# Unnormalised queries: the inverse query norm moves into the softmax's exponential and its bias, with new order words

## The reference, cut to what matters

```
q = l2norm(q) * qs;  k = l2norm(k) * ksc          # l2norm(t) = t / max(|t|, 1e-12), per token and head
q, k = rotary_xpos(q, k)                          # rotation and per-feature scale, linear in q and k
bq = q * 8.0                                      # QK_SCALE; windows of 64, keys of this and the window before
sim = where(mask, -finfo.max, einsum('bhwid,bhwjd->bhwij', bq, bk))
attn = softmax(sim);  out = einsum('bhwij,bhwjd->bhwid', attn, bv)      # 8 heads of 64 features
```

## Time and profile before

| what | value |
|---|---|
| median of three executions | 2480.55 us |
| range | 2479.12 to 2483.96 us |
| the profiled execution, first to last instruction | 2483.7 us |
| one pass with the pipeline full (997.9 to 1138.8 us) | 140.9 us |
| busy: PE, DVE, ACT, POOL | 1934.9, 1919.8, 1830.6, 1778.2 us |

### The profile page before, as it was taken

The page is one execution under the profiler, slowest core; times in us unless marked ns, Lnnn a source line. Parts: engine busy times, 40 slices in busy tenths (PEclk is TensorE's granted clock), DMA queues, the critical chain, the costliest instruction groups (busy, mean ns, idle before and its releaser), DMA issues.

```text
span 2483.7 us, 44331 instructions
## 1 busy us (share of the span) xinstructions
PE 1934.9 (78%) x15936; PEld 1113.3 (45%) x15936; DVE 1919.8 (77%) x3509; ACT 1830.6 (74%) x4051; POOL 1778.2 (72%) x1668
## 2 busy tenths in 40 slices
PE   2156788797878888797878879797888879787866
PEld 0013355353635445353635445363645445363634
DVE  3557797978879797988879797988879797977442
ACT  2255788787878878786878878797878878686634
POOL 1969595977959596977959596886959596883020
PEclk9767999999999999999999999999999999999978
DMA  4443423333434333434433333434433333330000
GB/s 163 123 120 98 112 74 104 98 96 103 103 111 104 100 89 95 102 90 115 104 107 95 107 86 91 106 91 116 112 106 95 106 88 91 102 90 9 6 5 9
DMA packets 116107, 231.27 MB, mean 93 GB/s; under 512 B 24880, under 2 KB 57648, under 8 KB 115632
## 3 DMA queue, kind: packets, MB, share of 16 engines
q1 hardware_dynamic: 115888, 228.44, 34.5%
HBM read 185.42 MB, written 42.99 MB: 92 GB/s over the span
## 4 chain that ended last, share of the span: by engine, by line
DVE 30%; PE 28%; ACT 19%; issue 12%; POOL 2%; DMA 1%; DVEq 0%; SPq 0%; POOLq 0%; ACTq 0%
DVE hs L617 9%; DVE m L885 5%; ACT late L850 3%; DVE kr L899 3%; ACT da L593 3%; DVE b_bank L889 3%; PE b_bank L341 3%; DVE f_bank L889 2%; PE b_bank L719 2%; PE f_bank L341 2%; DVE ss L872 2%; PE b_bank L764 2%; DVE mx L916 2%; PE f_bank L995 2%; PE f_bank L1001 2%
## 5 line engine op out<-in xcount | busy, mean ns | idle before, releaser
L617 DVE TENSOR_TENSOR_SCAN hs<-da,dbu 128x512 f32<-128x512 f32 x512 | 622.3, 1215 | 112.8 <-POOL dbu L645 85.4
L662 POOL TENSOR_TENSOR gy<-hs,bc 128x512 f32<-128x512 f32 x512 | 650.4, 1270 | 44.9 <-DVE hs L617 40.9
L645 POOL TENSOR_TENSOR dbu<-spread,bc 128x512 f32<-128x512 f32 x512 | 649.5, 1269 | 9.2 <-DMA spread<-steps 9.2
L593 ACT ACTIVATE da<-spread,rest 128x512 f32<-128x512 f32 x512 | 359.1, 701 | 163.3 <-DVE hs L617 143.9
L954 POOL TENSOR_TENSOR kr<-kr,rn 128x512 f32<-128x512 f32 x256 | 263.6, 1040 | 18.7 <-ACT rn L810 15.3
L693 PE MATMUL b_bank<-rest,h_t 128*128 128x512 f32 x384 | 225.1, 687 | 49.2 <-DVE kr L899 40.8
L693 PE MATMUL f_bank<-rest,h_t 128*128 128x512 f32 x384 | 217.4, 653 | 56.5 <-DVE kr L899 49.3
L570 PE MATMUL y_sum<-gy,rest 128*32 128x512 f32 x1024 | 144.2, 638 | 87.9 <-POOL gy L662 87.9
L341 PE MATMUL b_bank<-first,kr 128*128 128x128 f32 x768 | 131.7, 307 | 97.0 <-DVE kr L899 61.5
L341 PE MATMUL f_bank<-first,kr 128*128 128x128 f32 x768 | 125.1, 291 | 100.3 <-DVE kr L899 63.3
L1107 POOL TENSOR_TENSOR xs<-xs,v 128x512 f32<-128x512 f32 x16 | 18.9, 1184 | 229.6 <-ACT xs L336 229.6
(11 more groups left out here) (172 smaller groups left out, 4942.1 us busy)
## 6 DMA issues: line engine op xcount, KB each, us to landing
spread<-steps SPq DMA_DIRECT2D x256, 512.0 KB, 4.7
bc<-bc_rows SPq DMA_DIRECT2D x32, 512.0 KB, 6.8
steps<-k_t SPq DMA_DIRECT2D x32, 512.0 KB, 2.7
gate<-gates SPq DMA_DIRECT2D x32, 512.0 KB, 5.6
gates<-kr SPq DMA_DIRECT2D x16, 512.0 KB, 2.7
gates<-late SPq DMA_DIRECT2D x16, 512.0 KB, 3.4
sq<-in_x SPq DMA_DIRECT2D x16, 256.0 KB, 4.8
x<-in_x SPq DMA_DIRECT2D x16, 256.0 KB, 4.8
```

The source lines that it names most:

```text
L593: e.activation(da[:, :], spread[:, slot(b, s // 2), 0, :], ACT.Exp, scale=a_neg[:, s:s + 1]).then_inc(decayed.sem, 1)
L617: e.tensor_tensor_scan(hs[:, s % 2, :], da[:, :], dbu[:, s % 2, :], 0.0, ALU.mult, ALU.add).then_inc(scanned.sem, 1)
L645: e.tensor_tensor(dbu[:, s % 2, :], spread[:, slot(b, s // 2), 1, :], bc[:, s % 2, :], ALU.mult).then_inc(fed.sem, 1)
L662: e.tensor_tensor(gy[:, s % 8, :], hs[:, s % 2, :], bc[:, 2 + s % 2, :], ALU.mult).then_inc(read_out.sem, 1)
```

## The change

Queries are no longer multiplied by `rn` on POOL: the take list of `pool_attention` loses q0 to q3, and PE turns a query tile as soon as DVE's `add` (L899) has written it. The scores, and so the row maximum, are then too large by the query's norm over 8. ACT's exponential gets the inverse query norm as its per-partition scale. Its bias is a new tile `shift`, the negated maximum times the inverse norm, which DVE makes per head in a new `tensor_tensor` of 128x4 (both inputs and the output in SBUF; `shift` is a view of `lg`, by which name the order shows it). A new semaphore `shifted` takes the place of `peaked` before the exponential. DVE's attention stream has 8 steps more, POOL's 4 fewer, and all five order words are new.

```
 ORDER = {
     "pool": (
-        "F4 C1 A4 M1 B1 M1 B1 M2 B1 M1 B1 M2 B1 M1 B3 M1 A1 M1 A2 M1 B1 M1 A1 B1 M1 B2 M1 B1 A1 M2 B1 A1 B2 M4 A3 "
-        "M1 A1 M1 A1 M1 A1 M44"),
+        "F4 C1 A2 B1 M5 B2 M3 A1 M1 B3 M1 A1 M1 A1 B1 M1 A1 M1 B1 M1 A1 B1 M1 A1 M1 B3 M5 A1 M2 A1 M1 A2 M43"),
...
+                self.shift = self.lg[:, :, 0:NT]
...
-                self.rotated, self.added, self.normed = s("rotated", 16), s("added", 8), s("normed", 8)
+                self.rotated, self.added, self.normed = s("rotated", 16), s("added", 8), s("normed", 4)
+                self.shifted = s("shifted", 8)
...
-                    E.wait_ge(*w.normed(b, ROPE.index(take.lower())))
+                    E.wait_ge(*(w.normed(b, t) if kind == "K" else w.added(b, ROPE.index(take.lower()))))
...
-                E.wait_ge(*w.peaked(b, hd))
+                E.wait_ge(*w.shifted(b, hd))
...
                 for p in range(NT):
+                    n = ROPE.index(f"q{p}")
                     op = e.activation(w.pr[:, hd % 2, p, :], X[hd % 2][:, p * P:(p + 1) * P], ACT.Exp,
-                                      bias=w.mx[:, hd, p:p + 1])
+                                      bias=w.shift[:, hd, p:p + 1], scale=w.rn[:, n, hd:hd + 1])
...
                 e.tensor_reduce(w.mx[:, hd, :], X[hd % 2][:, :].rearrange("p (t k) -> p t k", t=NT), AX, ALU.max,
                                 negate=True).then_inc(w.peaked.sem, 1)
+                yield
+                E.wait_ge(*w.inverse(b, 2))
+                E.wait_ge(*w.peaked(b, hd))
+                inverse_q = w.rn[:, :, hd].rearrange("p (a k i) -> p k a i", a=2, k=2)[:, 0, :, :]
+                e.tensor_tensor(w.shift[:, hd, :].rearrange("p (a i) -> p a i", a=2),
+                                w.mx[:, hd, :].rearrange("p (a i) -> p a i", a=2), inverse_q, ALU.mult).then_inc(
+                    w.shifted.sem, 1)
+                yield
...
-            for take in "c0 q0 q1 v0 c1 k0 v1 k1 c2 q2 q3 v2 v3 c3 k2 k3".split():
+            for take in "c0 v0 c1 k0 v1 k1 c2 v2 v3 c3 k2 k3".split():
```

More of the change, by code:

```diff
@@ L44 @@
     "pe": (
[3 rows of a table removed]
[3 rows of a table added]
     "act": (
[4 rows of a table removed]
[4 rows of a table added]
     "dve": (
[4 rows of a table removed]
[4 rows of a table added]
     "pool": (
-        "F4 C1 A4 M1 B1 M1 B1 M2 B1 M1 B1 M2 B1 M1 B3 M1 A1 M1 A2 M1 B1 M1 A1 B1 M1 B2 M1 B1 A1 M2 B1 A1 B2 M4 A3 "
-        "M1 A1 M1 A1 M1 A1 M44"),
-    "sp": "M1 F2 M10 E1 M2 C1 M6 B1 M2 S1 M1 S2",
+        "F4 C1 A2 B1 M5 B2 M3 A1 M1 B3 M1 A1 M1 A1 B1 M1 A1 M1 B1 M1 A1 B1 M1 A1 M1 B3 M5 A1 M2 A1 M1 A2 M43"),
+    "sp": (
+        "M1 F2 M3 C1 M7 E1 M6 B1 M5 S3"),
 }
@@ L929, in dve_attention @@
             for hd in range(0, HEADS, 2):
[L930 to L933, removed]
+                yield from peak(hd)
+                yield from peak(hd + 1)
                 if hd:
```

## The result

The changed kernel takes 2677.7 us (median of 4, 2670.9 to 2678.9) against 2479.8 us. The ratio is 1.0784, with a 95% interval of 1.0767 to 1.0801. The profiled execution has a span of 2675.7 us. The forecast was slower, 2615 us with a range of 2495 to 2720, and the time lies in its upper part.

What follows compares the result with a forecast made beforehand. DVE and POOL were both held near their limit for 106 us of a 140.9 us pass. Product 41, wait 151, exponential 27, absorption -73 and relief -15 made +131 on 2484: 2615 us, range 2495 to 2720.

Steps and rivals of the forecast that it cites:

- the signs: What would show the forecast right or wrong: product duration, POOL's busy time and waits, exponential duration, rotation stretch and pass length.
- the 0.5 named: On DVE, beside POOL: the new product's mean would be 0.5 us or more if the forecast was right.
- the 0.8 of my value: On DVE: the new product's mean duration, 0.8 us, that goes with the wait of 0.65 us taken.
- 147 to 151: Whole pass: predicted length in us after the change, against 140.9 before.
- POOL's relief, 15 us gain: POOL: 128 normalisations go, 133 us of its time; only one per pass, behind the rotations, gives time back, 15 us.
- The product's own 41 us: DVE, between scans: 256 new 128x4 products at an undisturbed 0.16 us each add 41 us.
- Its wait, 151 us: DVE beside POOL: 232 products each wait 0.65 us for a POOL operation boundary; bounds 81 and 269 us.
- Rival (c): DVE heads: the product loses every boundary until POOL is dry, 190 to 290 us more, about 2740 us; chance 0.13.
- The exponential, 27 us: ACT: scale and bias per partition lengthen exponentials; L850's chain share grows 17 to 37 us, 27 taken; bounds 0 and 120.
- The absorption, 73 us: DVE's idle in a pass's first two parts takes up 5.0 us per pass, 73 us; bounds 49 and 99.
- the rotation stretch keeps its length: First 35 us of a pass, DVE busy 34.97 of 35.10: its length was to stay unchanged.
- The second way to the size: Gaps from scan 10 to 32: ten get products and grow, some 10 us per pass, less what POOL's idle returns.

Runs made afterwards that it cites:

- e1: Changed kernel with the DVE product replaced by a one-input copy of mx in the same place, exponential scale a column of ones: 2607.8 us, 1.050.
- e8: Changed kernel with the one-input copy for the product, constant exponential scale 1.0 and the order words of before: 2502.3 us, 1.0066.
- e6: Kernel before, all normalisations kept, plus the 128x4 DVE product of two SBUF tiles behind each row maximum, read as the exponential's bias: 2577.5 us, 1.0375.
- e7: Kernel before with a column of ones as the exponential's per-partition scale beside its bias: 2548.9 us, 1.0259.
- e3: Changed kernel, new order words kept, with the one-input copy for the product and constant exponential scale 1.0: 2572.8 us, 1.037.
- e2: Changed kernel with a constant exponential scale (0.0), the DVE product left as it is: 2663.8 us, 1.073.

## Why the prediction was right, and which terms were off

Its direction and its mechanism hold. Its sum has wrong sizes that partly cancel, and lacks a term. Each alone, in medians: relief -2, product +93, scale +64, which makes 2640 of 2484; the kernel with all three in the old order measures 2647, so they add up within 7 us, though the product's group is 26 us longer there than alone (159.6 against 133.5). The new words bring +31. In the prediction's terms that is 39 + 94 + 64 - 40 - 2 = +155, and 7 and 31 more make +193, where the forecast had 41 + 151 + 27 - 73 - 15 = +131. The wait was put 57 us too high, and the exponential, the absorption and the relief came out 37, 33 and 13 us dearer. That these leave only 24 us between them is luck and no merit of the terms.

Of the signs, the product's mean is 0.515 us, just above the 0.5 named and short of the 0.8 of my value; the 24 products behind the last scan take 0.13 to 0.17 us; POOL waits for scans for 170 us, and scans wait less for `dbu`. POOL's busy time falls by 119 us on the page (131 in the group of normalisations). A pass takes 153.5 us and not 147 to 151, and the stretch ahead of scan 10 doesn't keep its length.

- **POOL's relief, 15 us gain.** 2 us. The reason is shown: ahead of scan 10 nothing moves, since DVE is the limit there. The one normalisation behind it gave nothing either.
- **The product's own 41 us.** 256 x 0.153 = 39 us in e1. In the time, a one-input instruction in its place costs about 20 (18 in e8, less the relief's -2).
- **Its wait, 151 us.** The rule by which the time comes out is confirmed by 147 of 147 long products. The size was too large: 0.515-0.16 = 0.36 us each, 91 us in all (94 in e6, 119 with the old words), which is nearer to my low bound of 81 than to the middle. Of the 232 products that I let wait, 85 took under 0.2 us, 71 of them with POOL idle at their start, and only one clearly lost a boundary. Rival (c) is out with it.
- **The exponential, 27 us.** This is the term most off for its size: 64 alone. The per-instruction price was right (0.48 us forecast, 0.47 measured; 95 us more of ACT time), but I took its share from one line's part of the chain. In e7 the longer waits are those for `da`, the scores and the values, which stand under other names in the chain. My upper bound of 120 covered it. What it costs depends on what stands beside it: 64 us alone, 35 with the short copy and the new words, 14 with the full product and the new words.
- **The absorption, 73 us.** I took 73 off 192 us of DVE work for the product. In e6 it is 133.5 us of work and 93 of time, so 40 us are absorbed, and 25 of these because `mr_enter` no longer waits (31.3 us before, 5.8 in e6). So little of DVE's idle served as room. My reading, which no run tests by itself, is that much of that idle was the wait for the very chain that got longer.
- **The words.** No term, and 31 us. I had said that the rotation stretch keeps its length: in the old order it does, exactly; with the new words scan 10 is 2.4 us late. In that stretch `mr_out`, 0.15 us undisturbed, takes 0.94 us on average after. At 1057.61 it meets POOL's step for the next sequence. A row of DVE's timeline after:

```profile
1057.61 1.11 DVE L332 SCALAR_TENSOR_TENSOR mr_out<-mv_out,rs_out 128x4 f32<-128x4 f32 x1
```

And POOL's, two operations in one row, which end at 1058.70:

```profile
1056.21 2.49 POOL L423 TENSOR_TENSOR k_t<-k_t,late 128x512 f32<-128x512 f32 x2
```

Over the 16 `mr_out` that is 12.5 us on DVE. Whether they show in the time isn't shown: the mixture of words in which `mr_out` takes 0.154 us is no faster. What the 31 us are, and why it is 70 between e3 and e8, stays open. So does the lower granted clock of the profiled executions: 0.940 before, 0.910 after, 0.92 with the old words. Ahead of scan 10 it is 0.88 before and 0.83 after, in the windows shown. PE's projections, in two groups, take 0.72 and 0.74 us after and 0.65 and 0.69 before; with all the old words they take 0.65 and 0.69 beside the new operations too. So slower projections come with the new words, and the clock may be a part of what these cost. No run separates the two. Against a large part speaks that the changed kernel took 2677.5 us at 0.910 and 2678.0 at 0.928. The product's and the scale's costs were measured in the old order, at 0.936 and 0.928.

The second way to the size gave some 10 us per pass for the product alone. It is 5.1 (140.9 to 146.0 in e6). The scans there are up to 7.2 us late by scan 22, and 5.1 from scan 26 on, behind the `mr_enter` that no longer waits. In e6 204 of the 256 products end with a POOL operation, at 0.52 us on average, so it's the growth of the gaps that I had too large.

## What to carry to other kernels

Before moving work off an engine, leave that work out and time it: here 8 us per pass of an engine that was 95% busy in the stretch where most of them stood were worth 0.1%, since another engine was the limit there. What replaces it is priced by the chain it joins: a product that every head waits for, 0.16 us undisturbed and 0.52 beside POOL, and some 0.1 us on an exponential cost 93 and 64 us, though DVE and ACT were idle for 15 and 19% of each pass. A small DVE product with two SBUF inputs was charged the rest of POOL's operation here, and in some places further ones. The copy with one input in its place cost 20 us and not 93.

## What the runs showed of the hardware

The length of a small DVE product with two SBUF inputs followed POOL in all these traces: 0.13 to 0.17 us with POOL idle, otherwise until a POOL operation ended. In the kernel before, 9 of 16 `mr_enter` let two or three boundaries pass, with 3.0 us and more. Of 147 waiting products after, one did so clearly; with the old words it was 14 of 216, each 1.70 us long, and each time at the boundary between the copy of v and a `gy`. What decides who gets the next turn the runs don't show: the cases at 663.58 and 1085.50 start at the same point of a `dbu`, and one lost and the other didn't. A copy of the same 128x4 with one SBUF input took 0.153 us on average and never over 0.16, in 176 of 256 cases beside a running POOL operation. Per-partition scale beside a per-partition bias made an exponential of 128x128 from PSUM 0.09 us longer in itself (0.375 us with the bias from `lg` alone, in e2 and e6, 0.47 after), and a row of eight took 2.90 us instead of 2.17 before.
